# Second buffers for a layer's weights in the attention stage, and their loads moved from ScalarE's queue to SyncE's

## The reference, cut to what matters

```
def layer(h, p):
    wq, wk, bq_, bk_, l1w, l1b, l2w, l2b, l3w, l3b, w1, b1_, w2, b2_ = p
    q = (h @ wq.T + bq_).reshape(bh, sl, H, DH)        # 16 heads of 8
    k = (h @ wk.T + bk_).reshape(bh, sl, H, DH)
    scores = jnp.einsum('blhd,bmhd->bhlm', q, k) * inv_sqrt_d
    w_avg = jax.nn.softmax(scores, axis=-1).mean(axis=1)
    new_w = jax.nn.softmax(CSCALE * w_avg + rel[None], axis=-1)
    sa = jnp.einsum('blm,bme->ble', new_w, h)
    h1 = _ln(h + sa, l1w, l1b)
    h2 = _ln(h1, l2w, l2b)
    ff = jax.nn.relu(h2 @ w1.T + b1_) @ w2.T + b2_
    return (_ln(h2 + ff, l3w, l3b), None)
out, _ = jax.lax.scan(layer, x, (Wq, Wk, bq, bk, ...))  # 6 layers
```

## Time and profile before

| | |
|---|---|
| median of 3 runs | 2061.22 us (2057.03 to 2063.28) |
| profiled execution, its time | 2058.43 us |
| its span, first to last instruction | 2056.5 us |
| stage A | about 1130 us of it |
| busy: TensorE, VectorE, ScalarE, GpSimd | 86%, 81%, 78%, 60% of the span |
| mean granted TensorE clock | 0.950 |

### The profile page before, as it was taken

How to read it: one execution, slowest core, us unless ns; L and a number is a source line. 1 busy time by engine, 2 the same in 40 slices (tenths; PEclk the granted TensorE clock), 3 DMA queues, 4 the chain that set the end, 5 groups by cost and what they waited for, 6 DMA issues and landing times. The chain is left out here.

```text
span 2056.5 us, 37700 instructions
## 1 busy us (share of the span) xinstructions
PE 1762.6 (86%) x9830; PEld 1327.8 (65%) x9830; DVE 1661.3 (81%) x4303; ACT 1602.7 (78%) x5245; POOL 1224.6 (60%) x2106
## 2 busy tenths in 40 slices
PE   1788998899899889989989588669994999999996
PEld 0566776677677667767767456246562777777775
DVE  3799999999999999999998432768885788777784
ACT  1798999898899999999998223489971788888884
POOL 1267776777677677677777433359884555454450
PEclk8899999999999999999999699779997999999998
DMA  2222122122212222222220321012212000000000
GB/s 79 74 76 78 73 88 77 68 80 85 73 70 89 72 75 80 84 74 74 90 75 22 112 74 43 18 62 103 93 72 79 1 1 1 1 1 2 1 1 21
DMA packets 75299, 120.50 MB, mean 59 GB/s; under 512 B 10536, under 2 KB 59952, under 8 KB 67872
## 3 DMA queue, kind: packets, MB, share of 16 engines
q1 hardware_dynamic: 65920, 109.91, 15.3%
q10 hardware_dynamic: 7920, 5.60, 1.0%
q0 software_dynamic: 1248, 2.59, 0.4%
HBM read 95.44 MB, written 24.20 MB: 58 GB/s over the span
## 5 line engine op out<-in xcount | busy, mean ns | idle before, releaser
L436 ACT ACTIVATE a_prob<-a_scores,a_negmax 128x256 f32<-128x256 f32 x1536 | 706.5, 484 | 85.3 <-DVE a_negmax L538 57.9
L538 DVE TENSOR_REDUCE a_negmax<-a_scores 128x2 f32<-128x512 f32 x768 | 518.3, 675 | 43.5 <-PE a_scores L672 43.0
L684 PE MATMUL a_heads<-a_prob,a_diag 128*128 128x256 f32 x1920 | 478.2, 389 | 40.6 <-POOL a_diag L327 40.6
L327 POOL TENSOR_TENSOR a_diag<-ident,a_rowinv 128x256 f32<-128x256 f32 (+1 forms) x384 | 280.2, 735 | 248.7 <-DVE a_rowinv L592 243.5
L684 PEld LDWEIGHTS a_heads<-a_prob,a_diag 128*128 128x128 f32 x1920 | 358.3, 195 | 96.7 <-POOL a_diag L327 51.6
L672 PE MATMUL a_scores<-a_spread,a_spread 72*128 72x256 bf16 x1536 | 265.0, 276 | 92.9 <-ACT a_prob L436 53.9
L436 ACT ACTIVATION_READ_ACCUMULATOR a_prob<-a_scores,a_negmax 128x1 f32 x1536 | 330.9, 215 | 0.0
L672 PEld LDWEIGHTS a_scores<-a_spread,a_spread 72*128 72x128 bf16 x1536 | 127.6, 98 | 213.1 <-ACT a_prob L436 102.7
L1477 DVE TENSOR_TENSOR_SCAN c_state<-c_decay,c_psD 128x1024 f32<-128x1024 f32 x64 | 146.1, 2286 | 35.8 <-PE c_psD L1594 26.5
L1309 POOL TENSOR_TENSOR c_du<-c_state,c_c_row 128x1024 f32<-128x1024 f32 x64 | 151.3, 2365 | 30.3 <-DVE c_state L1477 21.2
L1933 ACT ACTIVATE d_prob<-d_psS,d_bias 128x128 f32<-128x128 f32 (+1 forms) x256 | 99.0, 396 | 35.5 <-DVE d_bias L2064 34.6
(11 more groups left out here) (291 smaller groups left out, 4111.4 us busy)
## 6 DMA issues: line engine op xcount, KB each, us to landing
a_spread<-a_split SPq DMA_DIRECT2D x48, 576.0 KB
a_spread<-a_split SPq DMA_DIRECT2D x144, 192.0 KB
a_split<-a_parts SPq DMA_DIRECT2D x48, 384.0 KB
c_c_row<-c_rows SPq DMA_DIRECT2D x32, 512.0 KB, 3.6
b_w<-in_b_w SPq DMA_DIRECT2D x1, 2816.0 KB, 14.9
a_w<-in_a_w ACTq DMA_DIRECT2D x10, 256.0 KB, 5.4
b_w<-in_b_w SPq DMA_DIRECT2D x1, 1536.0 KB, 17.9
d_wqkv<-in_d_wqkv SPq DMA_DIRECT2D x2, 768.0 KB, 5.8
```

Source lines behind the costliest of these rows:

```text
L327: g.tensor_tensor(diag[part % RING][:], ident[:].unsqueeze(1).broadcast_to([P, len(heads), P]), rowinv[part % RING][:, heads.start:heads.s ...
L436: ins = a.activation(prob[part % RING][:, c, :], psS[part % 2][:, c, :], ACT.Exp, bias=negmax[part % 2][:, c:c + 1], accum_out=rowsum[part ...
L538: v.tensor_reduce(negmax[part % 2][:, hs], psS[part % 2][:, hs, :], AX.X, ALU.max, negate=True).then_inc(s["negmax_ready"], 1)
L684: ins = p.matmul(psH[:, t, :], diag[part % RING][:, k, :], prob[part % RING][:, c, :], start=(j == 0 and k == 0), stop=(j == HG - 1 and c ...
```

## The change

All eleven tensors get a second buffer, taken by `lay % 2`. The loads of the next layer go into the buffer that the present layer doesn't use, so they needn't wait for the end of the layer: they stand behind the `spread` of sequences 3, 4 and 5, two groups each, and SyncE issues them. The semaphores they wait on are those of the layer before.

```diff
-            if q == SEQS - 1 and l + 1 < LAYERS:
-                for part, slot in enumerate((-10, 20, 25, 29, 32, 38)):
-                    place(at + slot, "load", l, q, part)
+            if 3 <= q < 6 and l + 1 < LAYERS:
+                for part in (2 * q - 6, 2 * q - 5):
+                    place(at - 9, "load", l, q, part)
...
-        wq = sb("wq", [P, P])
+        wq = two("wq", [P, P])
...
-                eng.dma_start(dst[:], d[name][l]).then_inc(s[signal], 16)
+                eng.dma_start(dst[l % 2][:], d[name][l]).then_inc(s[signal], 16)
...
+                    elif kind == "load":
+                        signal = groups[part][0]
+                        sp.wait_ge(s[signal], (lay + 1) * 16 * (len(groups[part]) - 1))
+                        n = lay * SEQS
+                        if lay and part == 0:
+                            sp.wait_ge(s["wqs_ready"], lay * 3)
+                            sp.wait_ge(s["split_step"], n * 6 - 5)
+                        elif lay and part == 1:
+                            sp.wait_ge(s["n1_ready"], n)
+                        elif lay and part == 2:
+                            sp.wait_ge(s["h2_ready"], n)
+                        elif lay and part == 3:
+                            sp.wait_ge(s["act_ready"], n * FC)
+                        elif lay and part == 4:
+                            sp.wait_ge(s["y_ready"], n)
+                        elif lay:
+                            sp.wait_ge(s["hT_ready"], n + SEQS)
+                            sp.wait_ge(s["h_tok_ready"], n + SEQS)
+                        load(sp, lay + 1, *groups[part])
...
-                    elif kind == "load":
-                        n = (lay + 1) * SEQS
-                        if part == 0:
-                            a.wait_ge(s["wqs_ready"], (lay + 1) * 3)
-                            a.wait_ge(s["split_step"], n * 6 - 5)
-                        elif part == 1:
-                            a.wait_ge(s["n1_ready"], n)
...
-                        load(a, lay + 1, *groups[part])
...
-                        for k, w in enumerate((wqs, wk)):
+                        for k, w in enumerate((wqs, wk[lay % 2])):
```

More of the change, by code:

```diff
@@ L198, in stage_a @@
         rel = sb("rel", [P, TPS, L])
-        wq = sb("wq", [P, P])
-        wk = sb("wk", [P, P])
-        qk_cols = sb("qk_cols", [P, 2])
+        wq = two("wq", [P, P])
+        wk = two("wk", [P, P])
+        qk_cols = two("qk_cols", [P, 2])
         wqs = sb("wqs", [P, P])
@@ L205, in stage_a @@
         one = sb("one", [P, 1])
-        rows1 = sb("rows1", [P, 2, E])
-        w1 = sb("w1", [P, HID_A])
-        rows2 = sb("rows2", [P, 3, E])
-        cols2 = sb("cols2", [P, 2])
-        b1 = sb("b1", [P, FC])
-        w2 = sb("w2", [P, FC, E])
-        rows3 = sb("rows3", [P, 2, E])
-        cols3 = sb("cols3", [P, 2])
+        rows1 = two("rows1", [P, 2, E])
+        w1 = two("w1", [P, HID_A])
+        rows2 = two("rows2", [P, 3, E])
+        cols2 = two("cols2", [P, 2])
+        b1 = two("b1", [P, FC])
+        w2 = two("w2", [P, FC, E])
+        rows3 = two("rows3", [P, 2, E])
+        cols3 = two("cols3", [P, 2])
         mb = [[{k: sb(f"{k}{n}_{u}", w) for k, w in (("st", [P, TPS, 6]), ("f", [P, TPS, 3]), ("mv", [P, 3, TPS]))}
@@ L316, in do @@
                         g.wait_ge(s["split_step"], lay * SEQS * 6)
-                        g.tensor_tensor(wqs[:], wq[:], qscale[:].broadcast_to([P, P]), ALU.mult)\
+                        g.tensor_tensor(wqs[:], wq[lay % 2][:], qscale[:].broadcast_to([P, P]), ALU.mult)\
                             .then_inc(s["wqs_ready"], 1)
-                        g.tensor_tensor(cols[:, 0:1], qk_cols[:, 0:1], qscale[:], ALU.mult).then_inc(s["wqs_ready"], 1)
-                        g.tensor_tensor(cols[:, 1:2], qk_cols[:, 1:2], one[:], ALU.mult).then_inc(s["wqs_ready"], 1)
+                        g.tensor_tensor(cols[:, 0:1], qk_cols[lay % 2][:, 0:1], qscale[:], ALU.mult).then_inc(s["wqs_ready"], 1)
+                        g.tensor_tensor(cols[:, 1:2], qk_cols[lay % 2][:, 1:2], one[:], ALU.mult).then_inc(s["wqs_ready"], 1)
                     elif kind == "diag":
@@ L357, in do @@
                         g.wait_ge(s["norm0"], m + 1)
[L358 removed]
+                        g.tensor_tensor(n1[u][:], r[u][:], rows1[lay % 2][:, 0:1, :].broadcast_to([P, TPS, E]), ALU.mult)\
                             .then_inc(s["gain1"], 1)
                         g.wait_ge(s["gain1"], m + 1)
[L361 removed]
+                        g.tensor_tensor(n1[u][:], n1[u][:], rows1[lay % 2][:, 1:2, :].broadcast_to([P, TPS, E]), ALU.add)\
                             .then_inc(s["n1_ready"], 1)
@@ L365, in do @@
                             g.wait_ge(s["norm2_in"], (lay + 1) * 16)
-                            g.tensor_tensor(rows2[:, 1, :], rows2[:, 1, :], rows2[:, 2, :], ALU.add)\
+                            gain2 = rows2[lay % 2]
+                            g.tensor_tensor(gain2[:, 1, :], gain2[:, 1, :], gain2[:, 2, :], ALU.add)\
                                 .then_inc(s["rows2_ready"], 1)
@@ L410, in do @@
                                 .then_inc(s["split_step"], 1)
-                    elif kind == "load":
-                        n = (lay + 1) * SEQS
-                        if part == 0:
-                            a.wait_ge(s["wqs_ready"], (lay + 1) * 3)
-                            a.wait_ge(s["split_step"], n * 6 - 5)
-                        elif part == 1:
-                            a.wait_ge(s["n1_ready"], n)
-                        elif part == 2:
-                            a.wait_ge(s["h2_ready"], n)
-                        elif part == 3:
-                            a.wait_ge(s["act_ready"], n * FC)
-                        elif part == 4:
-                            a.wait_ge(s["y_ready"], n)
-                        else:
-                            a.wait_ge(s["hT_ready"], n + SEQS)
-                            a.wait_ge(s["h_tok_ready"], n + SEQS)
-                        load(a, lay + 1, *groups[part])
                     elif kind == "exp":
@@ L459, in do @@
                         a.wait_ge(s["hidden_in"], (lay + 1) * 48)
-                        a.activation(h2T[u][:], src[:, 0, :], ACT.Identity, bias=cols2[:, 1:2], scale=cols2[:, 0:1])\
+                        a.activation(h2T[u][:], src[:, 0, :], ACT.Identity, bias=cols2[lay % 2][:, 1:2], scale=cols2[lay % 2][:, 0:1])\
                             .then_inc(s["h2T_ready"], 1)
@@ L467, in do @@
                             f = 2 * part + k
-                            a.activation(act[:, f, :], src[:, k, :], ACT.Relu, bias=b1[:, f:f + 1])\
+                            a.activation(act[:, f, :], src[:, k, :], ACT.Relu, bias=b1[lay % 2][:, f:f + 1])\
                                 .then_inc(s["act_ready"], 1)
@@ L473, in do @@
                         a.wait_ge(s["norm3_in"], (lay + 1) * 32)
-                        a.activation(hT[:, q * L:(q + 1) * L], src[:, 0, :], ACT.Identity, bias=cols3[:, 1:2],
-                                     scale=cols3[:, 0:1]).then_inc(s["hT_ready"], 1)
+                        a.activation(hT[:, q * L:(q + 1) * L], src[:, 0, :], ACT.Identity, bias=cols3[lay % 2][:, 1:2],
+                                     scale=cols3[lay % 2][:, 0:1]).then_inc(s["hT_ready"], 1)
                         a.wait_ge(s["hT_ready"], m + 1 + SEQS)
@@ L710, in do @@
                             f = 2 * part + k
-                            ins = p.matmul(dst[:, k, :], w1[:, f * P:(f + 1) * P], h2T[u][:], start=True, stop=True)
+                            ins = p.matmul(dst[:, k, :], w1[lay % 2][:, f * P:(f + 1) * P], h2T[u][:], start=True, stop=True)
                         ins.then_inc(s["t_full"], 1)
```

12 lines of the change are left out of this document (5 added, 7 removed).

## The result

| | before | after |
|---|---|---|
| median of 4 runs | 2062.25 us (2057.03 to 2068.46) | 2033.54 us (2031.37 to 2036.48) |
| profiled execution, its time | 2058.43 us | 2031.37 us |
| its span | 2056.5 us | 2029.5 us |
| mean granted clock | 0.950 | 0.963 |

The ratio of the times is 0.987, with a 95% interval of 0.9852 to 0.9889: 1.3% less time, a small gain that is clear of the noise. The forecast was 2038 us in a range of 2031 to 2049.

The account below looks back on a forecast made before the run. VectorE, ScalarE and TensorE, 90 to 95% busy, share a score ring with little slack; ScalarE's load issues hold it up. 2058.4 - 21.8 + 0.5 = 2037.1 us, stated as 2038, range 2031 to 2049.

Parts of the forecast that it names:

- The place: Stage A: group 0 and 5 load issues follow ScalarE's wait for its own activation, its queue empty, and delay exponentials.
- The size: Stage A's 39 sequences: removing the issues from ScalarE saves 21.8 us, 11 direct plus 10.8 from the clock.
- the clock part: Six of ten places: TensorE's clock falls after the pause, 1.8 us each, 10.8 us in all.
- The direct part: Pauses at full clock: 1.3 us per group 0 load, 0.9 per group 5, at five passages, 11 us.
- the eleven: Stage A windows holding 21.8 us of the excess, six at clock 0.93, five at 1.00, following group 0 or 5 loads.
- my 0.9 us for a group 5: Direct cost put on each passage's last load group, issued by ScalarE behind a wait for its own activation.
- (B): Rival: only the direct part returns, the clock falls as often for other reasons; 2047.9 us, chance 0.09.
- (E): Rival: nothing comes back, since ScalarE waits for `a_negmax` as the profile's releaser says; 2058.9 us, chance 0.04.
- (C): Rival: load batches hold SyncE's chain up 12.8 us a layer; 2060 us, at half that delay 2043; chance 0.08.
- (D): Slower rival: batches hold SyncE up 19.2 us a layer, every transfer late; 2110 us, chance 0.03.
- The first layer: Transfers have no slack there, so a batch outlasting one delays the next: 0.5 us lost once, bounds 0 and 4.1.
- all ten places: Stage A: one group 0 and one group 5 load at each of five passages; four of them kept the clock.

Follow-up runs that it names:

- e1_off_the_drain: Kernel before, single buffers, ScalarE still issuing; only load groups 0 and 5 moved to slots not behind ScalarE's wait for its own activation: 2038.84 us, ratio 0.9906.
- f3_under_exp: Changed kernel plus three unread 1 KB DMAs per sequence, issued by ScalarE behind four queued exponentials: 2044.43 us, ratio 0.9881.
- d3_three_issues: Changed kernel plus three unread 1 KB DMAs per sequence, issued by ScalarE behind the wait for its own activation: 2177.92 us, ratio 1.0527.
- d2_two_issues: Changed kernel plus two unread 1 KB DMAs per sequence, issued by ScalarE behind the wait for its own activation: 2119.32 us, ratio 1.0293.
- e3_two_groups: Changed kernel, but load groups 1 to 4 issued by ScalarE in their old slots, into second buffers: 2040.92 us, ratio 0.9925.
- e4_one_batch: Changed kernel with all eleven loads in one batch behind the transfer of sequence 5: 2035.46 us, ratio 0.9895.
- e6_act_mid: Changed kernel with the mid-layer loads issued by ScalarE behind queued exponentials in sequences 4, 5 and 6, none by SyncE: 2035.36 us, ratio 0.9876.
- e5_ballast_12: Changed kernel plus twelve unread 256 KB DMAs behind the loads of sequences 3, 4 and 5: 2172.74 us, ratio 1.0502.
- e2: Changed kernel's second buffers, but all loads issued by ScalarE in the old slots: 2055.07 us, ratio 0.9992.

## Why the prediction was right, step by step

**The place.** Right, and shown from both sides: e1_off_the_drain takes the issues away from the emptied engine, moves no other load, and gets 18.8 of 22.15 us; f3_under_exp and d3_three_issues put the same three DMAs in the two kinds of place, for 0.03 us and for 116.7. That the profile named VectorE and once a DMA as the releaser said nothing of the cause; the end of the last issue, 0.13 us ahead of the exponential, was the row to believe.

**The size.** The forecast took 21.8 us off stage A, the 39 sequences gave 22.15. Its two parts are not measured apart in the changed kernel. d2_two_issues gives the clock part as 1.7 us a fall, for my 1.8. The direct part has the right size in sum, but its attribution was off: "no window of groups 1 to 4 is among the eleven" was read as "they cost nothing". e3_two_groups finds 5.2 us with them in their old slots, through the late landing of `w2`. Before the change some of that lay in the windows that I gave to group 5. In e3, with no group 5 on ScalarE, four of these five windows still take 22.41 to 22.55 us; only the last falls, from the 22.52 of the earlier trace rows to 21.94. So my 0.9 us for a group 5 may hold a part that is the late `w2`, for which TensorE waited 1.1 us before the change; how much isn't separated. That only the emptied engine costs is shown for 18.8 us, not for all of the 22.15. That the sum still came out is partly luck: it was read from whole windows, and the change removes the late `w2` too, by loading it in the middle of the layer.

**The rivals.** (B), the clock falls anyway, is refuted: it fell in none of 39 sequences, in the changed kernel, in e1, e3, e4, e6 and f3. What would have made (B) right was a clock that falls without these pauses. That the issuer itself is worth nothing is right, as e6_act_mid shows with 852.94 us; but the issue time behind an emptied engine has a price, 0.56 us for one of 0.33 and 1.07 for three of 1.49 together, and the clock on top. (E), nothing comes back, is refuted by the result. For (C) and (D) the mechanism exists (e5_ballast_12), the price at this size is nil in steady layers (e4_one_batch, with all eleven loads behind one transfer, 853.03 us).

**The first layer.** I had 0.5 us of loss; the stretch of the 39 begins 0.67 us earlier, and the two waits behind the first batches are shorter than before (0.89 and 1.02 us for 1.57 and 1.26). But the third batch is followed by a new wait of 0.22 us, and from the first L605 to the fifth it is 88.28 us for 87.32. In e1, e2 and e6, which load nothing by SyncE there, the same distance is 86.6, 88.3 and 90.3 us, so it varies by more than my 0.5 without the batches. The term is neither confirmed nor refuted.

**The rest of the span.** The profile gives 27.0 us, and 3.9 of them are behind stage A, where the code is the same. Time of the profiled execution less its 39 sequences is 1183.5 us before and 1178.6 after; in e1 to e4 and e6_act_mid, whose code outside the loads is the same too, it is 1181.8 to 1185.9. So other executions of these same stages differ by some 7 us, the profile of after happened to be the lowest, and I count no part of this as an effect of the edit. So the part of the forecast that these runs confirm is the stretch of the 39; how near the whole kernel came is partly chance. In medians the change is worth 28.7 us here, and 22.0 for e4_one_batch, its nearest relative.

**The median.** Before, the median lay 2.8 and then 3.8 us above the profiled execution; I left open whether that is more fallen clocks at the four places that kept it. The after runs lie within 5.1 us of each other, those of before within 11.4, which fits, and all ten places falling would add 4 x 1.8 = 7.2 us. Kernels that keep the clock through the 39 in their traces lie closer too (e1, e3 and e4 within 7.5, 3.3 and 5.6 us) than those that don't (the 19 runs of before beside them within 17.3, e2 within 11.8), and in the trace of e2 five of the ten places fell for six. But no second trace of before was kept, so it stays an argument.

## What to carry to other kernels

An instruction that costs an engine's sequencer 0.3 us is free while the engine has queued work, and here cost 0.56 us right behind a wait for that engine's own result; before moving a load to another engine or buying a second buffer, look whether a slot two places away has queued work over it. Read what such a pause costs from whole windows between two instructions of the same kind, since the releaser that the profile names can be wrong and a fallen clock is spread over the matmuls behind it. When several loads near a transfer are late, look at the transfer: here its shape was worth 15 us, all of it in the first layer, where nothing covers a transfer.

## What the runs showed of the hardware that wasn't expected

- The clock answers to short added pauses in this loop: it fell in 1 of 39 sequences with an added TensorE pause of 0.48 us, in 33 with 0.96, in 36 with 1.63, each beside a normal handover wait of 0.44. With the change a wait of 1.0 us for `a_diag` in every sequence made it fall in none.
- One issue of 0.33 us behind the emptied engine took 0.56 us of a sequence, two took 0.59 and three 1.07. The second was nearly free where the clock stayed.
- A DMA of 256 KB that another queue issued near a narrow transfer landed some 9 us after its issue; with the transfer spread wider the waits for it fell from 3.8 to 0.9 us.
- SyncE's issues behind a transfer can stretch: with eleven loads, from about the fifth on, from 0.42 us to about 2, and in one case 7.04; with four loads, single ones to 1.47 and 1.68.
- The transfer on an outermost dimension of 8 went 1.9 times as fast as on 3.
